# One-core kernel for a weighted time sum, a sigmoid and a 1024x1024 product: the GpSimd sums by pairs of tiles, the split of the last t, and the places of loads and products

## The chip, the cores and the metric

The kernel runs on one core of a Trainium2 chip. The metric is the device time of one execution in microseconds. Lower is better.

## The reference

Inputs are x of 1024 x 24 x 1024 (batch, t, s) in float32, W1 of 1024 x 24, b1, W2 of 1024 x 1024 and b2.

```
h = sigmoid(einsum('bts,st->bs', x, W1) + b1)
y = h @ W2.T + b2
```

x has 100.7 MB and is read once; W2 has 4.2 MB, the output 4.2 MB.

## The kernel before

**Stages.** `STAGES` (L21) has four stages of 512 batch rows (four tiles of 128) by 512 columns of s (four chunks c): rows 0 to 511 with s 0 to 511, the same rows with s 512 to 1023, then both for rows 512 to 1023. In every stage the first 4 (stage 0) or 7 (the others) values of t go to GpSimd (POOL), the remaining 20 or 17 to TensorE (PE) and VectorE (DVE).

**The x path.** SyncE (SP) loads one t of a stage, 1 MiB, into one of five slots of `ring` (L277). `turn_unit` (L294) transposes the four tiles of one chunk into one of five PSUM banks `xbank` (L311); this is a unit, four per load. `add_unit` (L434) weighs the bank with W1's column and adds it to `acc` (L438; the first unit of a chunk writes `acc`, L432). A slot comes free when the last unit of the load is turned, a bank when its unit is added.

**Split loads.** The last t of stages 2 and 3 (6 and 8 of them) are loaded and turned in two parts: first tiles 0 and 1 of all of them, then tiles 2 and 3. A part is 512 KiB, its units have two transposes and 256 columns. So the sum of tiles 0 and 1 is complete earlier, and its product can begin.

**The POOL path.** A `part` is one t of two tiles, 512 KiB, loaded into one of seven slots of `nat` (L271). `weigh` (L602) multiplies it by a row of `w1all`, `add_sum` (L613) adds the slot of the same two tiles one t before. The order is stage, t, pair. After the last t the sum is transposed as a unit of kind "n" and added to `acc` (L436). In a stage without split it is one unit of four tiles per chunk, in a split stage two of two.

**The product.** `sigmoid` (L547) on ScalarE (ACT) gives h rounded (`h_hi`) and again in full in `hbank`; `low_part` (L448) on DVE makes the rest `h_lo`. An output half (128 rows x 512 columns) is 12 matmuls of 128 x 512 (`product_step`, L346, matmul L382), and one more for b2 in stages 0 and 2. ACT keeps the result of stages 0 and 2 in `y` (`keep_out`, L532); stages 1 and 3 are added to it by DVE (`add_out`, L467) and stored.

**Order.** Every engine runs its list in order. `STRETCHES` (L211) says how many product steps PE runs between which units: 104 of stage 0 in stage 1; 96 of stage 1 and 16 of stage 2 in stage 2; 88 of stage 2 and 36 of stage 3 in stage 3. 12 more (`REST`) run after the last unit; then come the 48 matmuls of the last four output halves (L415), which need the last sigmoids. `SETS` and `W2S` (L248, L252) say after which units W1's rows are spread and W2's tiles are turned (16 pieces, split by DVE, L445). SP's order is written in the places of `STAGES`: before which x load one part is loaded. SP waits for a slot of `nat` (L264, L266) and of `ring` (L276) before it issues, and everything behind it waits too.

Of the kernel before, what the change touches and what calls it, by code (L numbers as in the profile page):

```python
# [1 line left out]

# [8 lines left out]
P = 128  # L11
# [7 lines left out]


STAGES = (  # L21
    (0, 0, 4, 0, (2, 3, 5, 7, 9, 11, 12, 13, 15, 16, 17, 18), "keep"),
    (0, 4, 7, 0, (0, 3, 4, 5, 6, 8, 9, 10, 11, 12, 13, 14, 15, 16), "last"),
    (4, 0, 7, 6, (0, 3, 4, 5, 6, 8, 9, 10, 11, 12, 14, 17, 19, 21), "keep"),
    (4, 4, 7, 8, (0, 1, 3, 4, 5, 6, 8, 10, 12, 14), "last"),
)
# [4 lines left out]
def rec_kernel(nc, x, W1, b1, W2, b2, out):  # L31
# [10 lines left out]

    REST = 12

    CUT = JT // 2
# [3 lines left out]
    splits = [s[3] for s in STAGES]  # L49
    fate = [s[5] for s in STAGES]  # L50
    NK0, NK = pools[0], max(pools)
    HALF = JT // 2
# [9 lines left out]
    for i in range(NS):  # L62
        order = []
        for t, row, n in loads[i]:
            if t == T - 2 and row + n == JT:
                order += [("n", 0, c, row, n) for c in range(NC)]
            order += [("x", t, c, row, n) for c in range(NC)]
            if t == T - 1 and row + n < JT:
                order += [("n", 0, c, row, n) for c in range(NC)]
        units.append(order)  # L70
# [25 lines left out]

    parts = [(i, k, f) for i in range(NS) for k in range(pools[i]) for f in range(2)]
    first_part = [2 * sum(pools[:i]) for i in range(NS)]

    def sum_turned(i, f):  # L100

        return first_unit[i] + max(v for v, u in enumerate(units[i])
                                   if u[0] == "n" and u[3] < (f + 1) * HALF and u[3] + u[4] > f * HALF) + 1

    def sums_made(m):

        return m + 1 - 2 * (parts[m][0] + 1)

# [15 lines left out]
    x_v = x.rearrange("(j p) t s -> p j t s", p=P)  # L124
    out_v = out.rearrange("(j p) o -> p j o", p=P)
    w2_v = W2.rearrange("(h j p) s -> h p j s", p=P, j=JT)

    with ExitStack() as ctx:
# [13 lines left out]
        h_lo = sb("h_lo", [P, NC, BANK], F32R)  # L142
        w1all = sb("w1all", [P, NK, S])
        b2x = sb("b2x", [P, O], F32R)
        ones = sb("ones", [P, P], F32R)
        w1 = sb("w1", [P, SC * T])
        b1row = sb("b1row", [SC, P])
        b1col = sb("b1col", [P, SC])
# [53 lines left out]
        def part_end(i):  # L202
# [4 lines left out]

        AHEAD = 16
        LATE = 8
        HEAD = OH * CUT * steps_of(LAST)  # L210
        STRETCHES = (  # L211
            (OUTS * steps_of(0), first_unit[1] + 2 * NC, first_unit[1] + len(units[1]) * 4 // 5),
            (OUTS * steps_of(1), first_unit[2] + 2 * NC, part_end(2) + NC),
            (AHEAD, part_end(2) + 2 * NC, first_unit[3]),
            (OUTS * steps_of(2) - AHEAD - LATE, first_unit[3], part_end(3)),
            (LATE, part_end(3), part_end(3) + 2 * NC),
            (HEAD - REST, part_end(3) + 2 * NC, UNITS),
        )
        tiles_to = [0]
        for order in units:  # L220
            for unit in order:
                tiles_to.append(tiles_to[-1] + unit[4])

        def steps_due(u):
# [5 lines left out]
            return due  # L230

        def steps_to(outs):

            return sum(steps_of(g // OUTS) for g in range(outs))

        def out_end(g):
# [4 lines left out]
            return steps_to(g + 1)  # L241

        def outs_due(u):

            return sum(out_end(g) <= steps_due(u) for g in range((NS - 1) * OUTS + OH * CUT))

        EARLY, SETN = 1 + NK0, 1 + 2 * NK
        SETS = {4 + q: q for q in range(EARLY)}  # L248
        SETS.update({38 + 2 * q: EARLY + q for q in range(SETN - EARLY)})

        ROWS = [(0, k) for k in range(NK0)] + [(1, k) for k in range(NK)] + [(0, k) for k in range(NK0, NK)]
        W2S = {14 + 3 * m if m < SC else 58 + 3 * (m - SC): m for m in range(OH * SC)}  # L252

        @block.sync
        def _(sp):
            sp.dma_start(w1[:, :].rearrange("p (c t) -> p c t", t=T),
                         W1.rearrange("(c p) t -> p c t", p=P)).then_inc(w1_loaded, 16)
            m = 0
            for i, (j0, c0, _, _, places, _) in enumerate(STAGES):
                for at, (t, row, n) in enumerate(loads[i]):  # L260
                    if at in places:
                        s, k, f = parts[m]
                        if m >= NATS and parts[m - NATS][1] < pools[parts[m - NATS][0]] - 1:
                            sp.wait_ge(nat_added, sums_made(m - NATS + 2))  # L264
                        elif m >= NATS:
                            sp.wait_ge(unit_turned, sum_turned(parts[m - NATS][0], parts[m - NATS][2]))  # L266
# [12 lines left out]
                    if i == 0 and at == 1:  # L279
                        sp.dma_start(y[:, :, :], w2_v[0]).then_inc(w2_loaded[0], 16)  # L280
                    if i == 0 and at == 13:
                        sp.wait_ge(w2_turned, SC)
                        sp.dma_start(y[:, :, :], w2_v[1]).then_inc(w2_loaded[1], 16)
# [9 lines left out]
        def _(pe):  # L293
            def turn_unit(i, v):  # L294
                u = first_unit[i] + v
                kind, t, c, row, n = units[i][v]
                if u >= XBANKS:
                    pe.wait_ge(unit_added, u + 1 - XBANKS)
                end = first_part[i] + 2 * pools[i]
                if kind == "x":  # L300
                    use, sub, value = held[i, t, row]
                    if c == 0:
                        pe.wait_ge(x_loaded[use % RING][sub], value)
                elif c == 0:
# [283 lines left out]
        def _(pool):  # L588
# [13 lines left out]
            def weigh(m):  # L602

                i, k, f = parts[m]
                c0 = STAGES[i][1]
                row = w1all[:, k, c0 * P:(c0 + NC) * P].unsqueeze(1).to_broadcast([P, HALF, NC * P])
                slot = nat[:, m % NATS, :, :]
                pool.wait_ge(nat_loaded[m % NATS], 16 * (m // NATS + 1))
                if k == 0 and f == 0 and i < 3:
                    pool.wait_ge(set_kept, (EARLY, EARLY + NK, SETN)[i])  # L610
                nc.gpsimd.tensor_tensor(slot, slot, row, ALU.mult).then_inc(nat_weighed, 1)  # L611

            def add_sum(m):  # L613

                k = parts[m][1]
# [6 lines left out]
            for m, (_, k, _) in enumerate(parts):  # L622
                weigh(m)
# [23 lines left out]
```

## Time and profile before

| what | value |
|---|---|
| three runs, median (lowest to highest) | 313.44 us (313.18 to 313.95) |
| the profiled execution | 313.13 us, its span 311.2 us |
| granted TensorE clock, mean | 0.961 of full |
| busy PE, DVE, POOL, ACT | 258.5, 246.9, 221.6, 56.8 us |
| HBM read and written | 104.97 and 4.19 MB |

Busy time is the time in which an engine had an instruction running. In the rows further down "start" is in us from the span's start, the second number is how long; "x4" is the number of instructions merged, the bracket behind a row the idle time before it and what ended it. Instructions overlap their neighbours a little, so the distance of two starts is what one costs in a full queue.

### The profile page before, as it was taken

The numbers are of one execution on the slowest core, as the hardware profiler recorded it, in microseconds if no ns is written. First come the engines' busy times: TensorE is split into PE (matmuls) and PEld (weight loads), VectorE is DVE, ScalarE is ACT, GpSimd is POOL, SyncE is SP. The second block draws the span as 40 slices with busy tenths as digits, with TensorE's granted clock in tenths as the row PEclk, the third lists the DMA queues.
The fourth block names the chain that finished last, engine by engine and source line by source line (L and its number), as shares of the span: only waits on it lengthen the run. The fifth ranks groups of instructions, "written<-read, shape, count | busy, mean of one in ns | idle before, by whom it ended". The sixth has DMA issues, their size and how long they took to land.

```text
span 311.2 us, 4764 instructions
## 1 busy us (share of the span) xinstructions
PE 258.5 (83%) x1721; PEld 220.2 (71%) x1721; DVE 246.9 (79%) x420; ACT 56.8 (18%) x99; POOL 221.6 (71%) x101
## 2 busy tenths in 40 slices
PE   0847778738875999999779998899995999999995
PEld 0746767638764888888677776777774878788884
DVE  0719999628999878878999888799993788899833
ACT  4201223212245010101060000004140000041220
POOL 3109777925975999999959989997997999930000
PEclk9969999968998899999979999999998999999999
DMA  7999999999999999999999999999999999990113
GB/s 221 405 388 387 387 385 387 401 388 387 385 387 384 386 387 386 387 386 387 386 386 387 386 398 390 392 387 386 386 394 396 388 387 387 386 344 21 67 70 135
DMA packets 55179, 109.48 MB, mean 352 GB/s; under 512 B 3434, under 2 KB 3442, under 8 KB 55156
## 3 DMA queue, kind: packets, MB, share of 16 engines
q1 hardware_dynamic: 54560, 107.06, 93.5%
q10 hardware_dynamic: 596, 2.11, 1.7%
q8 instruction: 14, 0.23, 0.3%
q14 instruction: 9, 0.07, 0.1%
HBM read 104.97 MB, written 4.19 MB: 351 GB/s over the span
## 4 chain that ended last, share of the span: by engine, by line
PE 43%; DMA 34%; SPq 10%; DVE 7%; issue 4%; DVEq 0%
DMA ring<-in_r_x 34%; PE xbank L311 21%; PE pbank L382 17%; SPq L271 7%; DVE acc L438 4%; PE xbank L415 3%; SPq L277 3%; PE pbank L372 1%; DVE acc L432 1%; DVE w_lo L445 1%; DVE y L472 1%; PE pbank L340 0%; DVE acc L436 0%; PE pbank L329 0%; DVE h_lo L453 0%
## 5 line engine op out<-in xcount | busy, mean ns | idle before, releaser
L438 DVE SCALAR_TENSOR_TENSOR acc<-xbank,w,acc 128x512 f32<-128x512 f32 (+1 forms) x324 | 198.4, 653 | 43.5 <-PE xbank L311 38.6
L311 PE MATMUL xbank<-ident,ring 128*128 128x128 f32 x1136 | 178.5, 284 | 47.4 <-DMA ring<-in_r_x 36.6
L311 PEld LDWEIGHTS xbank<-ident,ring 128*128 128x128 f32 x1136 | 143.2, 146 | 80.6 <-DVE acc L438 28.9
L611 POOL TENSOR_TENSOR nat<-nat,w1all 128x1024 f32<-128x1024 f32 x50 | 118.8, 2378 | 45.2 <-DMA nat<-in_r_x 31.1
L620 POOL TENSOR_TENSOR nat<-nat 128x1024 f32<-128x1024 f32 x42 | 99.9, 2379 | 3.3
L382 PE MATMUL pbank<-w_hi,h_hi 128*128 128x512 f32 x112 | 50.7, 453 | 0.0
L382 PE MATMUL pbank<-w_lo,h_hi 128*128 128x512 f32 x112 | 50.7, 453 | 0.0
L382 PE MATMUL pbank<-w_hi,h_lo 128*128 128x512 f32 x112 | 45.6, 455 | 0.0
L554 ACT ACTIVATE h_hi<-acc,b1col 128x256 fp32r<-128x256 f32 (+1 forms) x24 | 13.6, 569 | 79.0 <-DVE acc L436 52.0
L540 ACT COPY y<-pbank 128x512 f32<-128x512 f32 x16 | 9.4, 587 | 86.3 <-PE pbank L382 85.9
L382 PEld LDWEIGHTS pbank<-w_lo,h_hi 128*128 128x128 f32 x112 | 21.6, 193 | 0.3
L382 PEld LDWEIGHTS pbank<-w_hi,h_hi 128*128 128x128 f32 x112 | 21.6, 193 | 0.2
L382 PEld LDWEIGHTS pbank<-w_hi,h_lo 128*128 128x128 f32 x112 | 19.9, 195 | 0.3
L432 DVE TENSOR_SCALAR acc<-xbank,w 128x512 f32<-128x512 f32 x16 | 11.8, 740 | 9.0 <-PE xbank L311 8.9
L515 ACT CAST w_hi<-pbank 128x512 fp32r<-128x512 f32 x16 | 9.4, 588 | 30.5 <-PE pbank L340 30.5
L562 ACT ACTIVATE hbank<-acc,b1col 128x256 f32<-128x256 f32 (+1 forms) x24 | 13.1, 545 | 5.3 <-DVE h_lo L453 3.8
L510 ACT COPY w1all<-pbank 128x512 f32<-128x512 f32 x14 | 8.2, 587 | 28.5 <-PE pbank L329 28.5
L453 DVE TENSOR_TENSOR h_lo<-hbank,h_hi 128x256 fp32r<-128x256 f32 (+1 forms) x20 | 10.4, 521 | 0.8 <-ACT hbank L562 0.2
L436 DVE TENSOR_TENSOR acc<-xbank,acc 128x256 f32<-128x256 f32 (+1 forms) x24 | 10.9, 503 | 0.0
L445 DVE TENSOR_TENSOR w_lo<-pbank,w_hi 128x512 fp32r<-128x512 f32 x16 | 10.9, 680 | 0.0
L340 PE MATMUL pbank<-ident,y 128*128 128x128 f32 x64 | 10.2, 284 | 0.7 <-DVE w_lo L445 0.7
L329 PE MATMUL pbank<-ident,w 128*128 128x128 f32 x56 | 9.4, 295 | 1.5 <-DVE w_lo L445 1.5
(30 smaller groups left out, 88.8 us busy)
## 6 DMA issues: line engine op xcount, KB each, us to landing
ring<-in_r_x SPq DMA_DIRECT2D x57, 1024.0 KB, 13.3
nat<-in_r_x SPq DMA_DIRECT2D x50, 512.0 KB, 13.0
ring<-in_r_x SPq DMA_DIRECT2D x28, 512.0 KB, 11.7
y<-in_L_rec_W SPq DMA_DIRECT2D x2, 2048.0 KB, 15.3
out_y<-y ACTq DMA_DIRECT2D x4, 512.0 KB, 6.7
out_y<-y SPq DMA_DIRECT2D x8, 256.0 KB, 2.0
w<-in_L_rec_W SPq DMA_DIRECT2D x1, 96.0 KB, 2.3
nat<-in_L_rec_b ACTq DMA_DIRECT2D x2, 4.0 KB
```

Of the source, the lines that this page charges most:

```text
L271: sp.dma_start(nat[:, m % NATS, :, :], x_v[:, sj:sj + HALF, k, sc * P:(sc + NC) * P]).then_inc(nat_loaded[m % NATS], 16)
L311: mm = pe.transpose(xbank[u % XBANKS][:, a * P:(a + 1) * P], tile, ident[:, :])
L382: mm = pe.matmul(pbank[n % 2][:, :], a[:, c, rows], w[:, STAGES[i][1] + c, cols], start=r == 0, stop=r == per - 1)
L432: nc.vector.tensor_scalar(total, bank, weight, None, ALU.mult).then_inc(unit_added, 1)
L436: nc.vector.tensor_tensor(total, bank, total, ALU.add).then_inc(unit_added, 1)
L438: nc.vector.scalar_tensor_tensor(out=total, in0=bank, scalar=weight, in1=total, op0=ALU.mult, op1=ALU.add).then_inc(unit_added, 1)
L445: nc.vector.tensor_tensor(w_lo[:, c, cols], pbank[m % 2][:, :], w_hi[:, c, cols].bitcast(F32), ALU.subtract).then_inc(w_lo_ready, 1)
L453: nc.vector.tensor_tensor(h_lo[:, c, rows], h_held(i, p), h_hi[:, c, rows].bitcast(F32), ALU.subtract).then_inc(h_lo_ready, 1)
L554: nc.scalar.activation(h_hi[:, c, rows], acc[:, c, rows], ACT.Sigmoid, bias=bias).then_inc(tail_hi if tail else h_hi_ready, 1)
L562: nc.scalar.activation(h_held(i, p), acc[:, c, rows], ACT.Sigmoid, bias=bias).then_inc(h_ready, 1)
L611: nc.gpsimd.tensor_tensor(slot, slot, row, ALU.mult).then_inc(nat_weighed, 1)
L620: nc.gpsimd.tensor_tensor(slot, slot, nat[:, (m - 2) % NATS, :, :], ALU.add).then_inc(nat_added, 1)
```

## The change

POOL's parts come in the order stage, pair, t: all t of tiles 0 and 1, then all t of tiles 2 and 3. Every stage turns each pair's sum as units of two tiles, placed by `STAGES` ahead of one given load. The splits of stages 2 and 3 grow from 6 and 8 to 11 and 12. The loads of the parts are placed anew, now also several ahead of one x load. `SPREAD` takes the place of `STRETCHES`: 104 steps of stage 0 in stage 1, 135 in stage 2 (96 of stage 1, 39 of stage 2), 105 in stage 3 (65 of stage 2, 40 of stage 3), 8 after the last unit. W1's rows and W2's tiles are turned earlier, W2's halves loaded behind load 0 and load 12 of stage 0 instead of 1 and 13. b1 is loaded into slot 5 of `nat`; `w1all` is laid out by halves.

```diff
+    (0, 0, 4, 0, (12, 14), (1, 3, 4, 4, 4, 4, 6, 6, 11, 13, 16, 19), "keep"),
+    (0, 4, 7, 0, (4, 15), (0, 2, 4, 6, 6, 7, 8, 8, 9, 9, 11, 14), "last"),
+    (4, 0, 7, 11, (12, 22), (0, 0, 2, 4, 4, 4, 6, 8, 12, 15, 20, 23, 23, 24, 27), "keep"),
+    (4, 4, 7, 12, (9, 28), (2, 2, 4, 7, 9, 10, 13, 18, 22, 24, 27), "last"),
+)
+
+SPREAD = (
+    (1, 2, 66, 104),
+    (2, 2, 49, 49),
+    (2, 58, 99, 33),
+    (2, 43, 120, 53),
+    (3, 4, 24, 33),
+    (3, 26, 65, 27),
+    (3, 67, 106, 25),
+    (3, 83, 121, 20),
 )
...
-        for t, row, n in loads[i]:
-            if t == T - 2 and row + n == JT:
-                order += [("n", 0, c, row, n) for c in range(NC)]
+        for at, (t, row, n) in enumerate(loads[i]):
+            order += [("n", 0, c, HALF * f, HALF) for f in range(2) if STAGES[i][4][f] == at for c in range(NC)]
             order += [("x", t, c, row, n) for c in range(NC)]
-            if t == T - 1 and row + n < JT:
-                order += [("n", 0, c, row, n) for c in range(NC)]
...
-    parts = [(i, k, f) for i in range(NS) for k in range(pools[i]) for f in range(2)]
+    parts = [(i, f, k) for i in range(NS) for f in range(2) for k in range(pools[i])]
...
-        STRETCHES = (
...
+        STRETCHES = [(steps, first_unit[i] + a, first_unit[i] + b) for i, a, b, steps in SPREAD]
...
-        SETS = {4 + q: q for q in range(EARLY)}
-        SETS.update({38 + 2 * q: EARLY + q for q in range(SETN - EARLY)})
+        SETS = {q: q for q in range(EARLY)}
+        SETS.update({37 + q: EARLY + q for q in range(SETN - EARLY)})
...
-        W2S = {14 + 3 * m if m < SC else 58 + 3 * (m - SC): m for m in range(OH * SC)}
+        W2S = {7 + 3 * m if m < SC else 50 + 3 * (m - SC): m for m in range(OH * SC)}
...
+                        if m == NATS - 2:
+
+                            sp.wait_ge(set_turned, 1)
...
                 elif c == 0:
-                    pe.wait_ge(nat_added, sums_made(end - 2 + (row + n - 1) // HALF))
+                    pe.wait_ge(nat_added, sums_made(last_part[i][row // HALF]))
...
-            act.dma_start(b1row[:, :], b1.rearrange("(c p) -> c p", p=P)).then_inc(b1_loaded, 16)
+            act.dma_start(nat[0:SC, NATS - 2, 0, 0:P], b1.rearrange("(c p) -> c p", p=P)).then_inc(b1_loaded, 16)
...
-                if k == 0 and f == 0 and i < 3:
-                    pool.wait_ge(set_kept, (EARLY, EARLY + NK, SETN)[i])
+                if f == 0:
+                    pool.wait_ge(set_kept, ROWS.index((STAGES[i][1] // NC, k)) + 2)
...
-                if k > 1:
-                    pool.wait_ge(nat_added, sums_made(m - 2))
-                nc.gpsimd.tensor_tensor(slot, slot, nat[:, (m - 2) % NATS, :, :], ALU.add).then_inc(nat_added, 1)
+                if parts[m][2] > 1:
+                    pool.wait_ge(nat_added, sums_made(m - 1))
+                nc.gpsimd.tensor_tensor(slot, slot, nat[:, (m - 1) % NATS, :, :], ALU.add).then_inc(nat_added, 1)
```

## Rows read from the trace of the kernel before

**Rows 1.** The page: what the DMA moved in each of 40 slices, and in all.

```profile
DMA  7999999999999999999999999999999999990113
GB/s 221 405 388 387 387 385 387 401 388 387 385 387 384 386 387 386 387 386 387 386 386 387 386 398 390 392 387 386 386 394 396 388 387 387 386 344 21 67 70 135
```

**Rows 2.** The chain that ended last, in order of time, its end.

```profile
258.20 11.64 DMA ring<-in_r_x
269.97 0.63 PE xbank L311 x4
...
294.20 2.98 PE pbank L382 x13
297.18 10.89 PE xbank L415 x48
```

**Rows 3.** Stretches of the last loads: us, PE, PEld, DVE, ACT, POOL busy (instructions), PEclk, DMA share, GB/s.

```profile
278.00:279.00 1.00, 1.00 (x10) 0.86 (x8) 1.00 (x4) 0.80 (x3) 0.00 (x0) 1.00 0.78 299
...
283.00:284.00 1.00, 1.00 (x8) 0.84 (x7) 1.00 (x4) 0.00 (x0) 0.00 (x0) 1.00 0.04 14
284.00:285.00 1.00, 1.00 (x8) 0.82 (x7) 0.85 (x3) 0.00 (x0) 0.00 (x0) 1.00 0.00 0
```

**Rows 4.** Timeline of SP's queue near the end.

```profile
258.20 15.15 SPq L277 DMA_DIRECT2D ring<-in_r_x  x11
```

**Rows 5.** The chain between 138 us and the end: two products, one unit of four.

```profile
138.06 0.46 PE pbank L382 x2
138.52 0.44 PE xbank L311 x4
```

**Rows 6.** Groups by line and form: DVE's units of x (two widths) and of the sums.

```profile
L438 DVE SCALAR_TENSOR_TENSOR acc<-xbank,w,acc 128x512 f32<-128x512 f32 x212 | 151.2, 747 | 40.6 <-PE xbank L311 36.0
L438 DVE SCALAR_TENSOR_TENSOR acc<-xbank,w,acc 128x256 f32<-128x256 f32 x112 | 47.2, 476 | 2.9 <-PE xbank L311 2.6
...
L436 DVE TENSOR_TENSOR acc<-xbank,acc 128x256 f32<-128x256 f32 x16 | 5.8, 414 | 0.0
```

**Rows 7.** Timeline of DVE: instructions in a full queue, one row of each kind.

```profile
93.82 0.69 DVE L453 TENSOR_TENSOR h_lo<-hbank,h_hi 128x512 fp32r<-128x512 f32 x1 [0.16 <-ACT hbank L562]
...
99.44 4.18 DVE L438 SCALAR_TENSOR_TENSOR acc<-xbank,w,acc 128x512 f32<-128x512 f32 x6
...
214.56 0.68 DVE L472 TENSOR_TENSOR y<-pbank,y 128x512 f32<-128x512 f32 x1
215.16 0.41 DVE L453 TENSOR_TENSOR h_lo<-hbank,h_hi 128x256 fp32r<-128x256 f32 x1
215.49 0.86 DVE L438 SCALAR_TENSOR_TENSOR acc<-xbank,w,acc 128x256 f32<-128x256 f32 x2
...
220.85 1.40 DVE L436 TENSOR_TENSOR acc<-xbank,acc 128x256 f32<-128x256 f32 x4
...
281.08 3.22 DVE L438 SCALAR_TENSOR_TENSOR acc<-xbank,w,acc 128x256 f32<-128x256 f32 x8
```

**Rows 8.** Timeline of POOL: its last part of t.

```profile
270.05 2.39 POOL L611 TENSOR_TENSOR nat<-nat,w1all 128x1024 f32<-128x1024 f32 x1
272.52 2.38 POOL L620 TENSOR_TENSOR nat<-nat 128x1024 f32<-128x1024 f32 x1
```

**Rows 9.** Timeline of PE: the idle time in stage 0 behind the second W2 load.

```profile
67.43 1.09 PE L311 MATMUL xbank<-ident,ring 128*128 128x128 f32 x4 [5.02 <-DMA ring<-in_r_x]
```

**Rows 10.** Stretches around PE's longest wait in the second half, columns as in rows 3.

```profile
236.00:239.00 3.00, 0.08 (x1) 0.11 (x2) 0.00 (x0) 0.00 (x0) 2.87 (x2) 1.00 1.05 396
...
240.00:241.00 1.00, 1.00 (x6) 0.80 (x5) 0.45 (x1) 0.00 (x0) 0.79 (x1) 0.50 1.07 393
...
243.00:244.00 1.00, 1.00 (x9) 0.90 (x8) 0.76 (x2) 0.59 (x1) 1.00 (x1) 1.00 1.07 393
```

**Rows 11.** Timeline of PE: that wait.

```profile
238.92 0.74 PE L311 MATMUL xbank<-ident,ring 128*128 128x128 f32 x4 [3.62 <-DMA ring<-in_r_x]
```

**Rows 12.** Timeline of ACT: the first sigmoid of stage 1.

```profile
155.23 0.72 ACT L554 ACTIVATE h_hi<-acc,b1col 128x512 fp32r<-128x512 f32 x1 [7.70 <-DVE acc L438]
```

More of the change, by code:

```diff
@@ L1 @@
 from contextlib import ExitStack
+from functools import cache
 import concourse.bass as bass
@@ L21 @@
 STAGES = (
[L22 to L25, printed above, removed]
+    (0, 0, 4, 0, (12, 14), (1, 3, 4, 4, 4, 4, 6, 6, 11, 13, 16, 19), "keep"),
[12 more added lines that the diff above has]
+    (3, 83, 121, 20),
 )
@@ L41, in rec_kernel @@
     XBANKS = 5
-    REST = 12
     CUT = JT // 2
@@ L49, in rec_kernel @@
     splits = [s[3] for s in STAGES]
-    fate = [s[5] for s in STAGES]
-    NK0, NK = pools[0], max(pools)
+    fate = [s[6] for s in STAGES]
+    NK0, NK1, NK2 = pools[0], max(pools[1], pools[3]), max(pools[0], pools[2])
     HALF = JT // 2
@@ L95, in rec_kernel @@
             use_end[use] = first_unit[i] + units[i].index(("x", t, NC - 1, row, n))
-    parts = [(i, k, f) for i in range(NS) for k in range(pools[i]) for f in range(2)]
-    first_part = [2 * sum(pools[:i]) for i in range(NS)]
+    parts = [(i, f, k) for i in range(NS) for f in range(2) for k in range(pools[i])]
+    last_part = [[2 * sum(pools[:i]) + (f + 1) * pools[i] - 1 for f in range(2)] for i in range(NS)]
     def sum_turned(i, f):
-        return first_unit[i] + max(v for v, u in enumerate(units[i])
-                                   if u[0] == "n" and u[3] < (f + 1) * HALF and u[3] + u[4] > f * HALF) + 1
+        return first_unit[i] + units[i].index(("n", 0, NC - 1, HALF * f, HALF)) + 1
     def sums_made(m):
-        return m + 1 - 2 * (parts[m][0] + 1)
+        return m + 1 - (2 * parts[m][0] + parts[m][1] + 1)
     def sum_end(i, p):
@@ L125, in rec_kernel @@
     out_v = out.rearrange("(j p) o -> p j o", p=P)
+    W2_LOADS = (0, 12)
     w2_v = W2.rearrange("(h j p) s -> h p j s", p=P, j=JT)
@@ L142, in rec_kernel @@
         h_lo = sb("h_lo", [P, NC, BANK], F32R)
-        w1all = sb("w1all", [P, NK, S])
+        w1all = sb("w1all", [P, NK1 + NK2, BANK])
         b2x = sb("b2x", [P, O], F32R)
@@ L146, in rec_kernel @@
         w1 = sb("w1", [P, SC * T])
-        b1row = sb("b1row", [SC, P])
         b1col = sb("b1col", [P, SC])
@@ L204, in part_end @@
             return first_unit[i] + max(v for v, u in enumerate(units[i]) if u[3] == 0) + 1
-        AHEAD = 16
-        LATE = 8
-        HEAD = OH * CUT * steps_of(LAST)
-        STRETCHES = (
[L212 to L218, printed above, removed]
+        STRETCHES = [(steps, first_unit[i] + a, first_unit[i] + b) for i, a, b, steps in SPREAD]
         tiles_to = [0]
@@ L222, in rec_kernel @@
                 tiles_to.append(tiles_to[-1] + unit[4])
+        @cache
         def steps_due(u):
@@ L230, in steps_due @@
             return due
+        @cache
         def steps_to(outs):
@@ L241, in out_end, with w1_row @@
             return steps_to(g + 1)
+        @cache
         def outs_due(u):
             return sum(out_end(g) <= steps_due(u) for g in range((NS - 1) * OUTS + OH * CUT))
-        EARLY, SETN = 1 + NK0, 1 + 2 * NK
-        SETS = {4 + q: q for q in range(EARLY)}
-        SETS.update({38 + 2 * q: EARLY + q for q in range(SETN - EARLY)})
-        ROWS = [(0, k) for k in range(NK0)] + [(1, k) for k in range(NK)] + [(0, k) for k in range(NK0, NK)]
-        W2S = {14 + 3 * m if m < SC else 58 + 3 * (m - SC): m for m in range(OH * SC)}
+        EARLY, SETN = 1 + NK0, 1 + NK1 + NK2
+        SETS = {q: q for q in range(EARLY)}
+        SETS.update({37 + q: EARLY + q for q in range(SETN - EARLY)})
+        ROWS = [(0, k) for k in range(NK0)] + [(1, k) for k in range(NK1)] + [(0, k) for k in range(NK0, NK2)]
+        def w1_row(half, k):
+            return w1all[:, NK2 * half + k, :]
+        W2S = {7 + 3 * m if m < SC else 50 + 3 * (m - SC): m for m in range(OH * SC)}
         @block.sync
@@ L258, in _ @@
             m = 0
-            for i, (j0, c0, _, _, places, _) in enumerate(STAGES):
+            for i, (j0, c0, _, _, _, places, _) in enumerate(STAGES):
                 for at, (t, row, n) in enumerate(loads[i]):
[L261 to L266, printed above, removed]
+                    for _ in range(places.count(at)):
+                        s, f, k = parts[m]
+                        if m >= NATS:
+                            back, half, step = parts[m - NATS]
+                            if step < pools[back] - 1:
+                                sp.wait_ge(nat_added, sums_made(m - NATS + 1))
+                            else:
+                                sp.wait_ge(unit_turned, sum_turned(back, half))
                         if m == NATS - 1:
                             sp.wait_ge(b2_ready, 1)
+                        if m == NATS - 2:
+                            sp.wait_ge(set_turned, 1)
                         sj, sc = STAGES[s][0] + HALF * f, STAGES[s][1]
@@ L278, in _ @@
                                  x_v[:, j0 + row:j0 + row + n, t, c0 * P:(c0 + NC) * P]).then_inc(x_loaded[use % RING][sub], 16)
-                    if i == 0 and at == 1:
+                    if i == 0 and at == W2_LOADS[0]:
                         sp.dma_start(y[:, :, :], w2_v[0]).then_inc(w2_loaded[0], 16)
-                    if i == 0 and at == 13:
+                    if i == 0 and at == W2_LOADS[1]:
                         sp.wait_ge(w2_turned, SC)
@@ L298, in turn_unit @@
                     pe.wait_ge(unit_added, u + 1 - XBANKS)
-                end = first_part[i] + 2 * pools[i]
                 if kind == "x":
@@ L309, in turn_unit @@
                     else:
-                        tile = nat[:, (end - 2 + (row + a) // HALF) % NATS, (row + a) % HALF, c * P:(c + 1) * P]
+                        tile = nat[:, last_part[i][row // HALF] % NATS, a, c * P:(c + 1) * P]
                     mm = pe.transpose(xbank[u % XBANKS][:, a * P:(a + 1) * P], tile, ident[:, :])
@@ L321, in turn_set @@
                     pe.wait_ge(b1_loaded, 16)
-                    pe.transpose(pbank[0][:, 0:SC], b1row[:, :], ident[0:SC, 0:SC]).then_inc(set_turned, 1)
+                    pe.transpose(pbank[0][:, 0:SC], nat[0:SC, NATS - 2, 0, 0:P], ident[0:SC, 0:SC]).then_inc(set_turned, 1)
                     return
@@ L509, in keep_set @@
                 half, k = ROWS[q - 1]
-                nc.scalar.copy(w1all[:, k, half * BANK:(half + 1) * BANK], pbank[q % 2][:, :]).then_inc(set_kept, 1)
+                nc.scalar.copy(w1_row(half, k), pbank[q % 2][:, :]).then_inc(set_kept, 1)
             def high_w2(m):
@@ L602, in weigh @@
             def weigh(m):
-                i, k, f = parts[m]
-                c0 = STAGES[i][1]
-                row = w1all[:, k, c0 * P:(c0 + NC) * P].unsqueeze(1).to_broadcast([P, HALF, NC * P])
+                i, f, k = parts[m]
+                row = w1_row(STAGES[i][1] // NC, k).unsqueeze(1).to_broadcast([P, HALF, BANK])
                 slot = nat[:, m % NATS, :, :]
                 pool.wait_ge(nat_loaded[m % NATS], 16 * (m // NATS + 1))
-                if k == 0 and f == 0 and i < 3:
-                    pool.wait_ge(set_kept, (EARLY, EARLY + NK, SETN)[i])
+                if f == 0:
+                    pool.wait_ge(set_kept, ROWS.index((STAGES[i][1] // NC, k)) + 2)
                 nc.gpsimd.tensor_tensor(slot, slot, row, ALU.mult).then_inc(nat_weighed, 1)
             def add_sum(m):
-                k = parts[m][1]
                 slot = nat[:, m % NATS, :, :]
                 pool.wait_ge(nat_weighed, m + 1)
-                if k > 1:
-                    pool.wait_ge(nat_added, sums_made(m - 2))
-                nc.gpsimd.tensor_tensor(slot, slot, nat[:, (m - 2) % NATS, :, :], ALU.add).then_inc(nat_added, 1)
-            for m, (_, k, _) in enumerate(parts):
+                if parts[m][2] > 1:
+                    pool.wait_ge(nat_added, sums_made(m - 1))
+                nc.gpsimd.tensor_tensor(slot, slot, nat[:, (m - 1) % NATS, :, :], ALU.add).then_inc(nat_added, 1)
+            for m, (_, _, k) in enumerate(parts):
                 weigh(m)
```

## The prediction

> **What bounds the kernel now.** I read first what the DMA moved. After the first slice no slice before the 36th falls below 384 GB/s [rows 1]: from about 8 to 278 us the transfers are the bound, and nothing that the engines do in that time can end the loads earlier. A half load of 0.524 MB takes 0.524 / 387 = 1.355 us of it. What a change can gain lies behind the loads.
>
> Next I read the end of the chain of waits. PE waits for a load a last time at 269.97 us. From there it runs without a break through 297.18, where the last 48 matmuls begin, and the span ends 14.1 us behind that, at 311.2 [rows 2]. The loads are in at 284: their rate falls from 278 on, 14 GB/s are left in the last microsecond [rows 3]; I read this fading as some of the 16 engines lagging behind the others, and a load is in when the slowest has its share. So 13 us pass between the end of the loads and the last 48 matmuls, filled with PE's backlog.
>
> Where the backlog is from is seen in the queue of SP: eleven half loads of x follow one another from 258.20 on, with no GpSimd part among them [rows 4]. In the code they are loads 14 to 24 of stage 3; the first is the one that PE took at 269.97. A transpose costs 0.44 / 4 = 0.11 us and a product 0.46 / 2 = 0.23 us [rows 5]. The eleven loads need 88 transposes, the sums 16 more, and the schedule places 67 products from there to the last 48 (steps 285 to 352): 104 x 0.11 + 67 x 0.23 = 11.4 + 15.4 = 26.8 us, which is just 269.97 to 297. The DMA brings these loads in 14.
>
> **The change, part by part.**
>
> *Steps moved.* Stage 2 gets 135 products instead of 112, stage 3 105 instead of 124, and 8 instead of 12 stay behind the last unit. PE's work is then, with 288 transposes a stage (31.7 us): stage 2 31.7 + 135 x 0.23 = 62.7 us (before 57.5), stage 3 31.7 + 105 x 0.23 = 55.8 us (before 60.2). The loads of a stage, 25.2 MB, take 65.0 us, and the stores of 2.1 MB add 5.4 us to the two stages together. PE now fits in both, in stage 2 with little to spare.
>
> *Loads placed anew.* The last twelve half loads now have four parts of POOL among them (before loads 18, 22, 24 and 27): 16 x 1.355 = 21.7 us. The work placed there is 12 x 8 + 8 = 104 transposes and 41 products (steps 303 to 344), 11.4 + 9.4 = 20.9 us. PE can follow the loads to the end. This is the main term: nearly the whole backlog goes.
>
> *More units of half width.* Of x, DVE gets 176 + 184 instead of 212 + 112 instructions of 512 and 256 columns (beside 16 first ones). Their listed means are 747 and 476 ns [rows 6], but in a full queue six wide ones take 4.18 us and eight narrow ones 3.22 us [rows 7]: 0.69 and 0.40 us each. The two halves cost 0.11 us more than the whole. The others by distance of starts [rows 7]: h_lo 0.33 (a wide one 0.69), y 0.60, a sum of a pair 1.40 / 4 = 0.35. Stage 2: 24 x 0.69 + 88 x 0.40 + 8 x 0.35 + 4 x 0.69 + 4 x 0.33 + 8 x 0.60 = 63.5 us (before, with 44 and 48, 61.3). Stage 3: 20 x 0.69 + 96 x 0.40 + 8 x 0.35 + 8 x 0.33 + 3 x 0.60 = 59.4 us. Together 122.9 us beside 135.5 us of DMA. I cost it at nothing in the end; cover gone, it is the slower rival below. In stages 0 and 1, eight units of a pair take the place of four wide ones, 0.4 us a stage, hidden by the DMA.
>
> *POOL.* Count and size of its 50 multiplications and 42 additions stay. The addition now needs the one before it on the same engine, which has ended long before; nothing. But the last part, issued ahead of load 27, now comes near the end, where before it was done at 274.9 [rows 8]. Two half loads follow it, so it lands 2.7 us ahead of the last, at 284 - 2.7 = 281.3. The bounds: 276.6 (the last bytes counted as if all engines ended together at 279.3) and 284 (with the last load). I take 281.3, since the slowest engine takes its share in order. A multiplication and an addition take 272.52 - 270.05 + 2.38 = 4.85 us [rows 8]: the sum is there at 286.1. POOL is free for it: the part before it has three half loads between, lands 4 x 1.355 = 5.4 us earlier and takes 4.85.
>
> *The new wait.* Units of the last sum stand ahead of load 28 in PE's list. Behind this wait are queued those four units, the four of load 28, and all products; DVE and the last sigmoids wait for them. From 286.1: 16 transposes and 2 products are 1.8 + 0.5 = 2.2 us, to 288.3; 8 products 1.8 us, to 290.1. DVE's eight units (4 x 0.35 + 4 x 0.40 = 3.0 us) end at 289.3, the first chunk's near 288, its sigmoid beside the 8 products, as before beside 12. The last 48 then begin at 290.1.
>
> *The beginning.* W1 and W2 pieces are turned earlier, the same number. PE comes to the second W2 half at unit 50, one load before it has been issued and with 2 MiB ahead of its landing. PE stands still for about 6 us there; before it stood still 5.02 us for the load behind W2 [rows 9]. What is queued behind: DVE, and the return of ring slots to SP. Five slots hold 5 x 2.7 = 13.5 us of x loads, parts add to that; a lag of 6 to 8 us leaves the DMA fed. I take nothing. If this cover is gone, each further microsecond counts in full. It could gain nothing, since the DMA is full now.
>
> *SP's waits.* The wait for b1's transpose ahead of part 5 is met after unit 0. Later parts wait for the addition six parts back; counted by the bytes ahead of each and 4.85 us of POOL a part, that addition ends 11 us (part 7) or more ahead of the due landing. The last loads need the slot of loads 17 and 18, free 15 us ahead. Nothing.
>
> **The sum.** Last 48 at 290.1 instead of 297.0 to 297.2, and the same 14.1 us behind: span 304.2. The profiled execution took 313.13 for 311.2, 1.9 more: 306.1 us; it is 0.3 below the median of the runs, so I say 306.2, 2.3% less than before. By the bounds of the landing: 276.6 leaves load 28 as the last thing (rival 1); 284 gives 288.9 for the sum, and 309.0 in all.
>
> **Rivals.** *1. The sum is not the last thing.* If the last part lands early, the units of load 28 run at 284: 8 transposes, 2 products 1.4 us, 8 products 1.8 us, last 48 at 287.3, 301.4 + 1.9 = 303.3 us. For it: PE and the DMA allow it. Against: landings lag behind the bytes.
>
> *2. PE comes late into stage 3.* Stage 2 is at 62.7 of about 67.7 us and PE and DVE wait for each other over five banks. If PE enters stage 3 as late as the ring lets it without hunger of the DMA, 9 us (an estimate: four slots are 10.8 us, less a load's own way) behind the first load (225.7, being 21.5 MiB or 58.3 us before 284), it works 55.8 + 0.9 us for the waits of DVE: 291.4, then 1.8 and 14.1: 307.3 + 1.9 = 309.2 us. Against it: the wait of 3 us at 236 to 239 [rows 10], slack that is there now.
>
> *3. The clock falls in the new wait.* PE is out of work about 2.4 us ahead of 286.1. Before 238.92 it stood still for 3.62 us [rows 11]; the granted clock went from 1.00 to 0.50, from 2.4 to 1.2 GHz, and was back at 243, some 3 us of work later [rows 10]. If that comes here, half of them, 1.5 us, are lost: 307.7 us. The Trainium skill (TensorE: Matmul & The Clock Gate, section "HAM oscillation — how this bites in real kernels") says that a matmul engine that stands idle over a DMA wait starts its next work at half rate; by that rule the time is this rival's. The trace agrees: the fall behind 236, and four transposes in 1.09 instead of 0.63 us behind the 5.02 us in stage 0.
>
> *4. DVE becomes the bound, slower.* If a narrow unit between products really costs its mean of 476 ns, and the rest their listed times too, stages 2 and 3 take 122.9 + 184 x 0.076 + 44 x 0.057 + 16 x 0.06 + 23 x 0.08 = 142.3 us of DVE [rows 6, 7]. Stage 1's sums are complete at 155.2, where the first sigmoid starts [rows 12], so the last unit is added at 297.5. PE, 0.3 us ahead of that, has 8 products to run: last 48 at 299.0, and 299.0 + 14.1 + 1.9 = 315.0 us, 0.6% slower. With the other prices as above it decides from 0.50 us a narrow unit on. For it: 0.476 is the mean of 112 [rows 6]. Against it: eight in 3.22 us [rows 7].
>
> **How the numbers follow.** The forecast has 0.50, rival 1 0.13, rival 2 0.16, rival 3 0.12, rival 4 0.09. The range must leave out rival 4 and little more: from below rival 1 to above rival 2, 302.5 to 309.8 us. A measurement of this kernel can tell 0.3% from no change, so "same" is 312.5 to 314.4. Rivals 1 to 3 and the forecast are all faster by more than that; of rival 4 a part is a tie. Faster 0.90, same 0.04, slower 0.06.
>
> **What would show it.** The DMA stays above 384 GB/s to the 36th slice; a lower slice in the first third would be slots that return late. The chain's end has GpSimd's last multiplication and addition between a load of nat and the transposes, near 281 to 286 us. PE waits for loads in the last 20 us, where it had no wait. The last 48 matmuls begin at 290 and take 10.9 us. A narrow unit stays at 0.40 us in a full queue. I am wrong if PE or DVE is busy without a break from 262 on, or if the loads end later than 285.

## The result, and the profile after

The changed kernel takes 308.94 us (median of four runs, 308.12 to 310.41), the kernel before beside it 313.38: ratio 0.9861, interval 0.9816 to 0.9905. It is faster, by 4.4 us where 7.2 were forecast, and inside the range. The profiled execution took 308.32 us for a span of 306.5.

The page, as in rows 1. The columns are 40 slices of the span.

```profile
DMA  7999999999999999999999999999999999997103
GB/s 211 404 388 386 386 388 385 401 387 386 388 387 386 387 389 385 386 387 387 386 387 387 387 391 391 396 388 386 386 384 396 392 388 385 384 385 271 44 36 137
```

The DMA is as full as before, to the 36th slice. Only the first slice is lower, 211 instead of 221 GB/s. Neither the beginning placed anew nor the new waits of SP left it hungry after that.

The end of the chain of waits, as in rows 2 (start, us, what):

```profile
273.56 2.40 POOL nat L622
275.96 0.07 issue
276.03 2.39 POOL nat L630
278.42 2.36 POOL nat L622
280.78 0.07 issue
280.85 2.39 POOL nat L630
283.24 0.05 POOL nat L622
...
288.14 0.63 PE xbank L323 x4
...
290.55 1.85 PE pbank L394 x8
292.39 10.90 PE xbank L427 x48
```

Before, this chain was PE's backlog; now it is GpSimd: six operations in a row from 273.56 to 288, the last three parts, and then the units, 8 products and the last 48 matmuls. These begin at 292.39, 4.8 us earlier than before, and the span is 4.7 us shorter. The whole gain lies ahead of them.

The loads end later than before. The issue of the last part of POOL (first row pair) and of the last load of x (second), as the view of single issues gives them:

```profile
L284 SPq DMA_DIRECT2D nat<-in_r_x x1: 471/471/471, 271.2 to 271.2; - x1
DMA to landing us min/median/max: 11.5/11.5/11.5
...
L290 SPq DMA_DIRECT2D ring<-in_r_x x1: 1229/1229/1229, 274.3 to 274.3; - x1
DMA to landing us min/median/max: 12.0/12.0/12.0
```

So the last part landed at 282.7 and the last load at 286.3. Before, the last load landed at 284.1.

Here is PE's and DVE's side of that wait, from the timeline:

```profile
285.60 0.68 DVE L484 TENSOR_TENSOR y<-pbank,y 128x512 f32<-128x512 f32 x1
285.65 2.35 POOL L630 TENSOR_TENSOR nat<-nat 128x1024 f32<-128x1024 f32 x1
286.19 1.26 DVE L450 SCALAR_TENSOR_TENSOR acc<-xbank,w,acc 128x256 f32<-128x256 f32 x3
...
288.14 0.63 PE L323 MATMUL xbank<-ident,nat 128*128 128x128 f32 x4 [2.31 <-POOL nat L630]
...
288.59 1.43 DVE L448 TENSOR_TENSOR acc<-xbank,acc 128x256 f32<-128x256 f32 x4 [1.14 <-PE xbank L323]
```

PE waited 2.31 us, DVE only 1.14. The stretches say why (window in us, its length, then busy PE, PEld, DVE, ACT, POOL, PEclk, DMA share, GB/s):

```profile
262.00:286.00 24.00, 23.16 (x158) 19.57 (x156) 24.00 (x62) 4.12 (x9) 17.62 (x9) 1.00 0.84 310
286.00:287.00 1.00, 0.00 (x0) 0.00 (x0) 1.00 (x4) 0.00 (x0) 1.00 (x1) 1.00 0.06 25
287.00:288.00 1.00, 0.00 (x0) 0.00 (x0) 0.45 (x2) 0.00 (x0) 1.00 (x1) 1.00 0.70 264
```

From 262 to 286 DVE had no gap at all. Three engines reach this point within 2.3 us of each other: PE was out of work at 285.8, DVE at 287.45, and GpSimd was done at 288.0. The 264 GB/s at 287 are a store of y.

The groups of DVE by form, as in rows 6:

```profile
L450 DVE SCALAR_TENSOR_TENSOR acc<-xbank,w,acc 128x512 f32<-128x512 f32 x176 | 123.0, 746 | 24.7 <-PE xbank L323 23.5
L450 DVE SCALAR_TENSOR_TENSOR acc<-xbank,w,acc 128x256 f32<-128x256 f32 x184 | 76.0, 476 | 2.5 <-PE xbank L323 2.3
```

The means are the old ones. In a full queue sixteen narrow units took 6.36 us, 0.40 us each, the price that the prediction used.

### The profile page after: what moved, and what is told of

Its sections match the earlier page's. It is cut to its first block, busy times and chain, and to the rows that moved or that the text cites. A ratio compares the mean times of both kernels' runs of the same rounds, so it can differ in the third digit from the quotient of the medians.

```text
span 306.5 us, 4894 instructions
## 1 busy us (share of the span) xinstructions
PE 258.5 (84%) x1721; PEld 220.2 (72%) x1721; DVE 248.6 (81%) x464; ACT 56.8 (19%) x99; POOL 221.7 (72%) x101
## 4 chain that ended last, share of the span: by engine, by line
POOL 45%; DMA 20%; issue 18%; PE 8%; DVE 3%; SPq 3%; ACT 1%; POOLq 1%; DVEq 0%; ACTq 0%
POOL nat L622 23%; POOL nat L630 22%; DMA nat<-in_r_x 9%; DMA y<-in_L_rec_W 6%; DMA ring<-in_r_x 5%; PE xbank L427 4%; PE xbank L323 3%; DVE acc L450 2%; SPq L290 2%; PE pbank L394 1%; PE pbank L352 1%; POOLq L139 1%; DVE w_lo L457 1%; ACT h_hi L566 0%; ACT L566 0%
## 5 line engine op out<-in xcount | busy, mean ns | idle before, releaser
L450 DVE SCALAR_TENSOR_TENSOR acc<-xbank,w,acc 128x256 f32<-128x256 f32 (+1 forms) x360 | 198.9, 608 | 27.3 <-PE xbank L323 25.8
L394 PE MATMUL pbank<-w_hi,h_lo 128*128 128x512 f32 x112 | 46.7, 457 | 0.0
L448 DVE TENSOR_TENSOR acc<-xbank,acc 128x256 f32<-128x256 f32 x32 | 12.2, 419 | 6.8 <-PE xbank L323 6.6
L352 PE MATMUL pbank<-ident,y 128*128 128x128 f32 x64 | 11.3, 304 | 5.2 <-DMA y<-in_L_rec_W 3.8
L323 PE MATMUL xbank<-ident,nat 128*128 128x128 f32 x64 | 10.6, 273 | 4.5 <-POOL nat L630 3.3
L574 ACT ACTIVATE hbank<-acc,b1col 128x256 f32<-128x256 f32 (+1 forms) x24 | 13.1, 545 | 6.3 <-DVE h_lo L465 5.3
L352 PEld LDWEIGHTS pbank<-ident,y 128*128 128x128 f32 x64 | 8.5, 157 | 6.3 <-DMA y<-in_L_rec_W 4.0
L323 PEld LDWEIGHTS xbank<-ident,nat 128*128 128x128 f32 x64 | 8.0, 141 | 6.5 <-DVE acc L450 5.3
```

Of the source, the lines that this page charges most:

```text
L352: mm = pe.transpose(pbank[m % 2][:, j * P:(j + 1) * P], y[:, j, c * P:(c + 1) * P], ident[:, :])
L394: mm = pe.matmul(pbank[n % 2][:, :], a[:, c, rows], w[:, STAGES[i][1] + c, cols], start=r == 0, stop=r == per - 1)
L448: nc.vector.tensor_tensor(total, bank, total, ALU.add).then_inc(unit_added, 1)
L450: nc.vector.scalar_tensor_tensor(out=total, in0=bank, scalar=weight, in1=total, op0=ALU.mult, op1=ALU.add).then_inc(unit_added, 1)
L574: nc.scalar.activation(h_held(i, p), acc[:, c, rows], ACT.Sigmoid, bias=bias).then_inc(h_ready, 1)
```

## The experiments

Each kernel was timed beside runs of the kernel before on the same chip; the ratios are to these. They were timed in three groups, each on another chip. "Mate" is a kernel timed in the same group; where a run has no mate, its median is set against 308.94 us and the ratios are the safer comparison.

### The changed kernel once more

> The changed kernel once more, as the mate of the runs beside it: 308 to 310.5 us, ratio to before 0.982 to 0.990. Every theory expects the last 48 matmuls to begin near 292.4 us in its trace.

308.94 us (308.3 to 309.91), ratio 0.9852, interval 0.9825 to 0.9878; its span was 306.5 us again.

### The last four parts earlier

```diff
-    (4, 4, 7, 12, (9, 28), (2, 2, 4, 7, 9, 10, 13, 18, 22, 24, 27), "last"),
+    (4, 4, 7, 12, (9, 28), (2, 2, 4, 7, 9, 10, 13, 17, 20, 22, 25), "last"),
```

> Only the last four GpSimd parts of stage 3 are loaded earlier (ahead of loads 17, 20, 22, 25 instead of 18, 22, 24, 27), so that the last sum is made some 2.7 us earlier. If the wait for GpSimd's last sum sets the end and PE is next (PE was out of work for 2.31 us there): 2.3 us faster than the changed kernel. If DVE is next (it was idle for only 1.14 us there and had been busy without a break since 262): 1.1 us faster. If the x loads, now closer together at the end, set it: no faster or slower.

307.40 us, ratio 0.9798, interval 0.9784 to 0.9813; repeated as a mate below 307.44, ratio 0.9801, 0.9787 to 0.9816. That is 1.5 us less than the changed kernel, the spans 0.9 less (305.6). The timeline of the first of the two:

```profile
287.46 0.83 PE L323 MATMUL xbank<-ident,nat 128*128 128x128 f32 x4 [0.17 <-DVE acc L450]
...
288.12 1.40 DVE L448 TENSOR_TENSOR acc<-xbank,acc 128x256 f32<-128x256 f32 x4
...
289.44 1.64 DVE L450 SCALAR_TENSOR_TENSOR acc<-xbank,w,acc 128x256 f32<-128x256 f32 x4
...
290.45 1.08 PE L394 MATMUL pbank<-w_hi,h_lo 128*128 128x512 f32 x4
```

The last sum is made at 285.2 and the wait for it is gone. PE now waits for DVE, and DVE is busy for 23.69 of the 23.80 us from 267.21 to 291.01. The last 48 begin at 291.53, 0.9 us earlier than in the changed kernel. So DVE was next in line, not PE: of PE's 2.31 us no more than DVE's 1.14 could be had. The runs also lie closer together, within 0.5 us (0.7 when repeated) instead of 1.6 to 2.3; the medians are 1.5 us apart and the profiled spans 0.9 because of that spread.

> The kernel with the last four parts earlier once more, as the mate of the runs beside it: 307.0 to 307.6 us, ratio to before 0.978 to 0.982.

### All parts of stage 3 early

```diff
-    (4, 4, 7, 12, (9, 28), (2, 2, 4, 7, 9, 10, 13, 18, 22, 24, 27), "last"),
+    (4, 4, 7, 12, (9, 28), (2, 2, 4, 5, 6, 8, 9, 11, 13, 15, 16), "last"),
```

> Of stage 3 the GpSimd parts are loaded as early as before the change (the last ahead of load 16), so that the last twelve half loads follow one another without a part. Theory C, as predicted (parts among the last loads give PE time to follow): the backlog comes back, PE needs 20.9 us for 16.3 us of loads, and the time is 1 to 4 us longer. Rival: PE and DVE are so nearly full in the last 24 us that they only trade a wait for the sum against a backlog, the same within 1 us, or up to 1 us faster since the wait for the sum goes.

311.08 us, ratio 0.9916, interval 0.9899 to 0.9933: 2.1 us slower than the changed kernel. Stretches:

```profile
262.00:270.00 8.00, 4.86 (x34) 3.97 (x34) 5.01 (x12) 0.00 (x0) 7.84 (x4) 1.00 1.04 378
270.00:278.00 8.00, 8.00 (x55) 6.62 (x54) 7.76 (x21) 4.13 (x9) 7.84 (x5) 1.00 1.04 384
278.00:286.00 8.00, 8.00 (x55) 6.73 (x53) 8.00 (x20) 0.00 (x0) 1.79 (x1) 1.00 0.39 144
286.00:294.00 8.00, 7.78 (x54) 6.31 (x53) 8.00 (x22) 0.00 (x0) 0.00 (x0) 1.00 0.18 67
```

GpSimd is done at 280, earlier than anybody needs it. PE and DVE idle for 3 us before 270, PE for want of x loads, and then both are full to the end. A backlog is back: the last 48 begin at 295.65. That crowded x loads leave work behind is thereby shown. Whose work it is differs from the prediction, which counted PE's alone. By its prices PE's 112 transposes and some 45 products from 269.79 to 293.80 are 22.7 of the 24.0 us, and the pieces between them in the chain of this run are DVE's additions (`DVE acc L450`).

### The steps as before

```diff
-    (2, 2, 49, 49),
-    (2, 58, 99, 33),
-    (2, 43, 120, 53),
-    (3, 4, 24, 33),
-    (3, 26, 65, 27),
-    (3, 67, 106, 25),
-    (3, 83, 121, 20),
+    (2, 8, 76, 96),
+    (2, 80, 120, 16),
+    (3, 0, 72, 80),
+    (3, 72, 80, 8),
+    (3, 80, 124, 36),
```

(The first entry is (1, 8, 60, 104).) In the changed kernel:

> The product steps are put where they were before: 112 instead of 135 in stage 2, 88 instead of 60 ahead of the end of the first part of stage 3, 12 instead of 8 behind the last unit. Theory A (the gain is from steps moved out of stage 3 into stage 2's slack): 24 to 28 products of 0.23 us come back into a stretch without slack, 4 to 6 us slower than the changed kernel, all of the gain gone. Theory B (the gain is from the loads and the larger splits, the steps matter little): at most 1 us slower.

311.36 us, ratio 0.9917, interval 0.9895 to 0.9940: 2.4 us slower than the changed kernel. The same with the last parts earlier:

> The last parts earlier and the product steps where they were before (112 in stage 2, 88 ahead of the end of stage 3's first part, 12 behind the last unit). There is no wait for the sum here, so the clock should not fall at the end. Theory A (the steps' places are worth their number only behind the last unit, since DVE sets the pace before it): 4 more products behind the last unit, 0.9 us more than the mate, 308.2 to 308.4. Theory B (PE's backlog of 28 products comes through): 4 us and more, above 311.

309.02 us, ratio 0.9848, interval 0.9834 to 0.9863: 1.6 us slower than its mate. The chain has

```profile
290.38 2.77 PE pbank L392 x12
293.15 10.89 PE xbank L425 x48
```

so 2.77 - 1.85 = 0.9 us are the four more products behind the last unit, and some 0.7 us are left for the products that the old steps place earlier in stage 3. These are 19 more ahead of the last unit (124 instead of 105), 16 of them by the end of the stage's first part; the 28 of the expectation sets 88 against 60 at different units. By their number they are 4.4 us of PE, and a sixth of that shows in the time. PE had gaps to take them: in the changed kernel it is busy for 19.11 of the 21 us before 262, here for 20.51.

In the run with the late parts, the first of the two, something else is added:

```profile
286.00:287.00 1.00, 0.00 (x0) 0.00 (x0) 1.00 (x3) 0.00 (x0) 1.00 (x1) 1.00 0.35 129
287.00:288.00 1.00, 0.21 (x3) 0.25 (x3) 0.09 (x1) 0.00 (x0) 0.64 (x1) 1.00 0.00 0
288.00:289.00 1.00, 1.00 (x7) 0.77 (x6) 0.74 (x2) 0.00 (x0) 0.00 (x0) 0.77 0.00 0
289.00:290.00 1.00, 1.00 (x6) 0.95 (x5) 0.59 (x3) 0.00 (x0) 0.00 (x0) 0.50 0.00 0
```

PE waited 1.92 us for GpSimd's sum, until 287.79. Some 0.7 us after it had resumed, the granted clock fell to 0.50, and it stayed there until 292. Half of these 3.5 us, about 1.7, are lost. This is rival 3, in a neighbour of the changed kernel, so the 2.4 us are not the price of the steps alone; the 1.6 us without this wait are the better measure.

### The splits as before

```diff
-    (4, 0, 7, 11, (12, 22), (0, 0, 2, 4, 4, 4, 6, 8, 12, 15, 20, 23, 23, 24, 27), "keep"),
-    (4, 4, 7, 12, (9, 28), (2, 2, 4, 7, 9, 10, 13, 18, 22, 24, 27), "last"),
+    (4, 0, 7, 6, (9, 17), (0, 0, 2, 4, 4, 4, 6, 7, 9, 10, 15, 18, 18, 19, 22), "keep"),
+    (4, 4, 7, 8, (9, 24), (2, 2, 4, 6, 7, 8, 9, 14, 18, 20, 23), "last"),
...
-    (2, 2, 49, 49),
-    (2, 58, 99, 33),
-    (2, 43, 120, 53),
-    (3, 4, 24, 33),
-    (3, 26, 65, 27),
-    (3, 67, 106, 25),
-    (3, 83, 121, 20),
+    (2, 2, 40, 49),
+    (2, 44, 78, 47),
+    (2, 80, 100, 39),
+    (3, 4, 30, 33),
+    (3, 31, 72, 32),
+    (3, 76, 106, 40),
```

> The changed kernel with splits of 6 and 8 instead of 11 and 12 t; loads of parts at the same bytes, products again 135 and 105 a stage, 40 of stage 3 in its shorter second part. Theory A (the larger splits pay, since stage 3's own products find 12 instead of 8 half loads beside them): PE needs 17.1 us of work for some 16.2 us of loads behind a fuller first part, 1 to 3 us slower than the changed kernel. Theory B (DVE sets the last 24 us, each t kept whole saves it 0.44 us): 4 t whole in stage 3 and 5 in stage 2 save it 1.8 and 2.2 us, 1 to 2 us faster.

310.77 us, ratio 0.9913, interval 0.9895 to 0.9930: 1.8 us slower than the changed kernel. PE has its last wait for a load ahead of 257.48 and is nearly full from then on (from 262 to 286 it is busy for 23.77 us, DVE for 23.56). With ten t instead of twelve in stage 3 alone, beside the earlier parts:

```diff
-    (4, 4, 7, 12, (9, 28), (2, 2, 4, 7, 9, 10, 13, 17, 20, 22, 25), "last"),
+    (4, 4, 7, 10, (10, 26), (2, 2, 4, 6, 8, 9, 11, 15, 18, 20, 23), "last"),
...
-    (3, 4, 24, 33),
-    (3, 26, 65, 27),
-    (3, 67, 106, 25),
-    (3, 83, 121, 20),
+    (3, 4, 26, 33),
+    (3, 28, 68, 29),
+    (3, 70, 102, 23),
+    (3, 80, 114, 20),
```

> Stage 3 split at 10 instead of 12 t, its last GpSimd parts at the bytes of the run with earlier last parts (307.4 us). If DVE sets the end: 2 t kept whole save 0.9 us of DVE, 0.5 to 0.9 us below that run, 306.5 to 306.9. If the product's place beside the loads is worth more: above 307.4.

308.23 us, ratio 0.9833, interval 0.9818 to 0.9848: 0.8 us more than with twelve (1.0 by the ratios), though DVE has 0.9 us less to do. From 280 to the end the chain holds PE's pieces alone. Both runs agree with this reading: a larger split gives stage 3's own products more loads to lie beside, and that is worth more than DVE's price for halves.

### The kernel before, with its last part late

```diff
-    (4, 4, 7, 8, (0, 1, 3, 4, 5, 6, 8, 10, 12, 14), "last"),
+    (4, 4, 7, 8, (0, 1, 3, 4, 5, 6, 8, 10, 12, 20), "last"),
```

> The kernel before with one edit: the last GpSimd part of stage 3 is loaded ahead of load 20 instead of 14 (with the old order only this one can come that late, the sum of tiles 0 and 1 needs the part before it). If the backlog is made by x loads that come too close together, the six half loads behind it come 1.4 us earlier, PE starts on its last stretch of 26.8 us earlier, and the time is 1.0 to 1.4 us below before. If PE or DVE was full ahead of that stretch too: no difference.

312.68 us, ratio 0.9977, interval 0.9966 to 0.9988: 0.8 us less, a little under the expected 1.0 to 1.4. PE's last wait for a load ends at 258.43 instead of 269.97, 11.5 us earlier, but the last 48 begin at 296.93, only 0.25 us earlier. Before, PE stood still ahead of 269.97 for just 0.68 us, and between 257.82 and there it had no other wait. So its backlog reached back to 258, further than the prediction looked, and 0.7 us was all that earlier loads could give. By the code the old order cannot go further, since the sum of tiles 0 and 1 needs all parts but this one ahead of load 16.

### The beginning as before

```diff
-    W2_LOADS = (0, 12)
+    W2_LOADS = (1, 13)
-        SETS = {q: q for q in range(EARLY)}
-        SETS.update({37 + q: EARLY + q for q in range(SETN - EARLY)})
+        SETS = {4 + q: q for q in range(EARLY)}
+        SETS.update({38 + 2 * q: EARLY + q for q in range(SETN - EARLY)})
-        W2S = {7 + 3 * m if m < SC else 50 + 3 * (m - SC): m for m in range(OH * SC)}
+        W2S = {14 + 3 * m if m < SC else 58 + 3 * (m - SC): m for m in range(OH * SC)}
```

> The changed kernel with W1's rows, W2's tiles and W2's loads placed as before. As predicted they are hidden by the DMA: the time of the changed kernel within 0.5 us, though PE's clock falls in another place of stage 0. Rival: the 8.4 us wait in stage 0 of the changed kernel costs something later: 1 us faster or more.

309.19 us, ratio 0.9866, interval 0.9849 to 0.9882: no difference from the changed kernel beyond the noise.

### Two attempts to go further

```diff
-    (3, 83, 121, 20),
+    (3, 83, 121, 24),
```

> The last parts earlier, and 4 instead of 8 products behind the last unit, the other 4 among the last units. If PE has room there (it was busy for 22.9 of 24 us before 286) because DVE sets the pace, and the first sigmoid is ready: up to 0.9 us below the mate, 306.4 to 307.0. If the last sigmoids or PE set it: the same as the mate, 307.2 to 307.6.

307.42 us, ratio 0.9799, interval 0.9785 to 0.9814: nothing. The last 48 begin at 291.23 instead of 291.57, but take 11.16 instead of 10.90 us. Their first weight load waits for the first sigmoid of ACT, which in turn waits for DVE's sum:

```profile
290.63 0.51 ACT L566 ACTIVATE h_hi<-acc,b1col 128x256 fp32r<-128x256 f32 x1 [18.78 <-DVE acc L450]
...
291.19 0.76 PEld L427 LDWEIGHTS xbank<-w_hi,h_hi 128*128 128x128 f32 x4 [0.40 <-ACT h_hi L566]
```

The second:

```diff
-    (4, 4, 7, 12, (9, 28), (2, 2, 4, 7, 9, 10, 13, 17, 20, 22, 25), "last"),
+    (4, 4, 8, 12, (10, 27), (1, 2, 3, 4, 6, 8, 10, 12, 14, 16, 18, 20, 22), "last"),
...
-    (3, 4, 24, 33),
-    (3, 26, 65, 27),
-    (3, 67, 106, 25),
-    (3, 83, 121, 20),
+    (3, 2, 22, 33),
+    (3, 24, 64, 27),
+    (3, 66, 102, 25),
+    (3, 79, 117, 20),
```

> GpSimd takes 8 instead of 7 t in stage 3, two more parts of 4.8 us, DVE 8 narrow units fewer, 3.2 us, PE 1.8 us less. If GpSimd's idle time in stage 3 (about 10 us) can hold the two parts: 1 to 3 us below the mate. If not, its last sum comes after 288 and PE waits for it again: the mate's time or up to 3 us more.

308.24 us, ratio 0.9828, interval 0.9812 to 0.9844: 0.8 us more than the mate. GpSimd is in time (its last sum at 286.5), but two more parts among the x loads push these back, and PE waits for them between 262 and 271 (0.94, 1.16 and 0.91 us). DVE is full again at the end.

## Why the prediction was right, and where it was short

**What bounds.** Right. The DMA stayed full, and the last 48 and what follows took 14.1 us as before. Between the last landing and the last 48 lay 13.1 us before (284.1 to 297.2) and lie 6.1 us now (286.3 to 292.4). That is 7.0 us less, of which the loads took 2.2 back by ending later.

**Loads placed anew.** The mechanism is right: taking it back alone costs 2.1 us and brings a backlog back. But the prediction counted the work behind the loads for PE alone, and from 262 on DVE was the fuller engine. Its size was taken too large as well, since two other parts give the rest.

**Steps moved.** The step "PE's backlog goes with the products" was worth less than their number: 1.6 us without the wait for the sum, 0.9 of them from the four behind the last unit.

**More units of half width.** I cost them at nothing "in the end", with DVE at 122.9 us beside 135.5 us of DMA. The price of one was right (0.40 us), but the cover was not there: an average over two stages hid that the last 24 us hold the densest DVE work, where DVE was busy for 24.00 us. The same sum made for the last twelve half loads alone (48 units of x, four of the sum, four h_lo, three y) gives 19.2 + 1.4 + 1.3 + 1.8 = 23.7 us for 21.7 us of loads. I made that sum for PE and not for DVE. The run with earlier parts shows what this is worth: with the sum made at 285.2, ahead of the forecast's 286.1, the last 48 began at 291.53 and not at 290.1. These 1.4 us are the larger share of the shortfall.

**POOL.** The sum was due at 286.1 and came at 288.0, 1.9 us late. The landings had the larger share. The last part was taken to land at 281.3, because the loads were to end at 284 as before; it landed at 282.7, and they ended at 286.3. Counted back from 281.3 by the loads between (five half loads of x and two parts, 7 x 1.355 = 9.5 us), part 47, the third from last, was due at 271.8; it landed at 273.5. "POOL is free for it" was wrong too, though by little. Parts 47 and 48 have two half loads between them, 4.1 us for 4.8 us of work, so three parts run in a row. From 271.8 they would have ended at 286.3, 0.2 us behind the forecast; from 273.5 they end at 288.0.

Why the loads end 2.2 us later is not shown. The first load of x landed 0.7 us later than before (8.2 instead of 7.6 us), and SP issued the first store of y at 278.45, among the last landings, where before it was issued at 289.20, behind them.

**The new wait.** Right in its place and its queue. Its length was 2.31 us for PE, where 2.4 was forecast, but that is luck: both of its ends came 2 us late. PE was out of work at 285.8 and not at 283.7, the sum was there at 288.0 and not at 286.1.

**The sum.** 304.2 was forecast for the span and 306.5 came, 2.3 us more. Read along the path, 1.9 us are the sum's lateness and 0.4 the way from the sum to the last 48 (4.4 us instead of 4.0). Read by what an early sum gives back, 0.9 us are the sum's and 1.4 are DVE's. The median, 308.94 us, lies another 0.6 above the profiled execution. So the forecast fell short by 2.7 us of its 7.2, and the time lies nearer to rival 2's 309.2 than to the forecast's 306.2, though that rival's mechanism did not occur.

**The signs.** Two that the prediction named as showing it wrong came: DVE was busy without a break from 262 on, and the loads ended later than 285. The first marks the step that put DVE's extra work at nothing, the second the landing of the last part.

**The beginning, and SP's waits.** The run that took the beginning back shows no effect on the time within the noise. SP's new waits are in every run of the new order and were not tested alone.

**Rivals.** Rival 1 did not occur; the run with earlier parts shows that DVE takes the sum's place before load 28 can. Rival 2 (PE late into stage 3) did not: PE waited for loads until 268.23. Rival 3 did not occur in three profiled executions with this wait (2.31, 2.28 and 2.30 us, clock 1.00 through it), and did behind a wait of 1.92 us in the run with the old steps. The Trainium skill (TensorE: Matmul & The Clock Gate, section "HAM oscillation — how this bites in real kernels") describes work that starts at half rate behind a wait for a DMA. The trace of the run with the old steps shows such a fall behind a wait for GpSimd, and the three others show none. Whether the slower executions of the changed kernel had it is open: two of its four have mean granted clocks of 0.972 (308.12 and 308.32 us) and two of 0.956 (309.56 and 310.41 us), but in the run with the old beginning the fastest execution has the lowest clock (308.13 us, 0.955). Rival 4 (DVE the bound) came true in kind and not in price: DVE sets the pace of the last 24 us, at 0.40 us a unit and not at 0.48, and costs part of the gain instead of all.

**What stays open.** The parts taken back one by one cost 2.1, 2.4 and 1.8 us, 6.3 in all, where the change gains 4.4; with 1.6 for the steps it is 5.5. They share the same gaps, and no run splits them further. No run takes back the new order of GpSimd's parts, or the sums turned as units of two tiles, by itself.

## What to carry to other kernels

Work that can only follow a stream of loads should be spread over the last loads by their time, for every engine that takes part: make the sum for the last 20 us, engine by engine, not for a stage. Of a helper engine with long operations count the last three in a row, not the last one: here its result came 14.5 us behind the landing of the third from last. Do not take the end of the loads from the kernel before without asking what else is stored or loaded beside them. When a gain was read as one engine's backlog, ask which engine ends second: here DVE waited only 1.1 us for GpSimd's sum, and making the sum 2.8 us earlier gave 0.9.

## What was not expected of the hardware

PE's clock fell behind a wait of 1.92 us (from 1.00 to 0.50 for some three microseconds) in one kernel and did not behind 2.31, 2.28 and 2.30 us in others. With the wait gone, the spread of the runs went from 1.6 to 2.3 us down to 0.5 and 0.7.

The last loads land evenly against the count of their bytes, though the rate in the page fades. In the changed kernel the half loads and parts from 266.7 to 277.6 land 1.33 to 1.36 us apart, where the DMA moves 387 GB/s. From there to 284.0, while the rate falls from 371 to 25 GB/s, they still land 1.26 to 1.33 us apart; only the last one comes 2.3 us behind.
